# Adjacency layer on one core: contiguous loads, the diagonal found by its column, and three changed orders

## What is computed

```python
x: (8192, 512) float32;  adj: (8192, 8192) float32, symmetric pattern, about 9 entries in a row, diagonal always present
h = relu(layernorm(x))
mask = (adj > 0)
head = mask / max(sqrt(sum(mask * mask, axis=-1)), 1e-12)
inc = adj + head
out = x + (inc @ h) / sum(inc, axis=-1)
```

## Time and profile before

| | before |
|---|---|
| median of 3 runs | 1271.77 us |
| span of the profiled execution (the profile gives no other time of it) | 1276.7 us |
| VectorE busy | 1189.2 us, 93% |
| ScalarE busy | 975.5 us, 76% |
| TensorE busy | 959.0 us, 75% |
| GpSimd busy | 791.1 us, 62% |
| DMA | 471 MB, 369 GB/s over the span |

### The profile page before, as it was taken

The page is one execution under the profiler, slowest core; times in us unless marked ns, Lnnn a source line. Parts: engine busy times, 40 slices in busy tenths (PEclk is TensorE's granted clock), DMA queues, the critical chain, the costliest instruction groups (busy, mean ns, idle before and its releaser), DMA issues.

```text
span 1276.7 us, 14660 instructions
## 1 busy us (share of the span) xinstructions
PE 959.0 (75%) x2680; PEld 478.1 (37%) x2682; DVE 1189.2 (93%) x2868; ACT 975.5 (76%) x1902; POOL 791.1 (62%) x748
## 2 busy tenths in 40 slices
PE   0003878888888878787988887978878888977677
PEld 0001434444444444443434443434444434433343
DVE  6679999998999999998999999999999999999961
ACT  6657787887887988786888877888877888884731
POOL 1003667676666777776766767777776776765562
PEclk9999899898988989899898989999989988987888
DMA  9999999999999999999999999999999999997532
GB/s 356 427 422 406 396 394 388 369 387 369 379 378 382 401 373 401 395 401 394 402 400 401 392 374 384 399 400 395 402 396 402 402 397 373 401 390 275 175 106 74
DMA packets 148207, 471.00 MB, mean 369 GB/s; under 512 B 24826, under 2 KB 24826, under 8 KB 143965
## 3 DMA queue, kind: packets, MB, share of 16 engines
q1 hardware_dynamic: 90368, 331.38, 66.3%
q0 software_dynamic: 57744, 138.64, 29.7%
HBM read 490.47 MB, written 33.82 MB: 411 GB/s over the span
## 4 chain that ended last, share of the span: by engine, by line
DVE 55%; issue 17%; DMA 11%; ACT 6%; PE 6%; another core or an unknown queue 2%; SPq 1%; POOL 0%; DVEq 0%; ACTq 0%; POOLq 0%
DVE cand_word L794 17%; DVE folded L772 16%; DMA adj_tile<-in_adj_dram 8%; DVE cand_index L798 6%; DMA gathered_rows<-in_x_dram 3%; PE acc L1326 3%; DVE cand_index L817 2%; DVE cand_word L812 2%; ACT junk L573 2%; ACT adj_tile L560 2%; ACT diag L636 1%; PE acc L1337 1%; DVE diagonal_alone L779 1%; DVE entry L961 1%
## 5 line engine op out<-in xcount | busy, mean ns | idle before, releaser
L494 POOL DMA_INDIRECT gathered_rows<-h_scratch,slot_column x520 | 559.9, 1077 | 263.1 <-issue 158.0
L573 ACT ACTIVATE junk<-adj_tile,zero_unit 128x2048 bf16<-128x2048 f32 x256 | 510.0, 1998 | 48.3 <-issue 27.5
L1326 PE MATMUL acc<-gathered_rows,diag 128*128 128x512 f32 x1040 | 489.6, 622 | 21.4 <-DMA gathered_rows<-h_scratch,slot_column 18.2
L494 POOL DMA_INDIRECT gathered_rows<-h_scratch,spill_column x198 | 223.1, 1127 | 195.0 <-ACT spill_column L619 135.2
L794 DVE MAX8 cand_word<-folded 128x8 f32<-128x1024 f32 x244 | 298.2, 1222 | 5.9 <-remote 1.3
L772 DVE SCALAR_TENSOR_TENSOR folded<-adj_tile 128x1024 f32<-128x1024 f32 x244 | 296.1, 1214 | 7.7 <-DMA adj_tile<-in_adj_dram 5.6
L1326 PEld LDWEIGHTS acc<-gathered_rows,diag 128*128 128x128 f32 x1040 | 203.8, 204 | 263.4 <-issue 262.6
L798 DVE FIND_INDEX8 cand_index<-cand_word,folded 128x8 uint32<-128x1024 f32 x244 | 297.3, 1219 | 0.0
L1337 PE MATMUL acc<-gathered_rows,spill_matrix 128*128 128x512 f32 x396 | 186.8, 609 | 46.0 <-DMA gathered_rows<-h_scratch,spill_column 42.4
L636 ACT ACTIVATE diag<-ident,weights_and_payload 128x128 f32<-128x128 f32 x581 | 176.2, 388 | 16.0 <-issue 6.5
L1337 PEld LDWEIGHTS acc<-gathered_rows,spill_matrix 128*128 128x128 f32 x396 | 72.8, 192 | 154.8 <-issue 154.6
(11 more groups left out here) (151 smaller groups left out, 880.1 us busy)
## 6 DMA issues: line engine op xcount, KB each, us to landing
adj_tile<-in_adj_dram SPq DMA_DIRECT2D x256, 1024.0 KB
h_scratch<-adj_tile SPq DMA_DIRECT2D x16, 1024.0 KB, 10.6
out_dram<-out_tile SPq DMA_DIRECT2D x64, 256.0 KB
gathered_rows<-in_x_dram SPq DMA_DIRECT2D x12, 1024.0 KB, 12.6
x_residual<-in_x_dram SPq DMA_DIRECT2D x48, 256.0 KB
gathered_rows<-h_scratch,slot_column POOLq DMA_INDIRECT x520
x_held<-in_x_dram SPq DMA_DIRECT2D x4, 1024.0 KB, 7.9
gathered_rows<-h_scratch,spill_column POOLq DMA_INDIRECT x198, 3.5
```

The lines of the kernel that those rows point to most:

```text
L494: nc.gpsimd.indirect_dma_start(out=into, out_offset=None, in_=h[:, :], in_offset=bass.IndirectOffsetOnAxis(ap=column, axis=0), bounds_chec ...
L573: nc.scalar.activation(junk[:, n % 2].rearrange("p (j c) -> p j c", j=2), both[:, :, half], ACT.Relu, bias=zero_unit[:], scale=-UP, accum_ ...
L1326: last = nc.tensor.matmul(acc[t % 3][:], diag[:, t % 2, 1 + s], slot(t % 2, s), start=False, stop=False)
```

## The change

1. A chunk is now 2048 columns that lie together, so each row gives one run of 8 KB. What is folded is the first 1024 of them with the second 1024. SyncE no longer waits for the reading of the diagonal before it reloads a chunk.
2. `read_diagonal`, `cut_diagonal` and `keep_diagonal` are gone. `find_diagonal` compares the columns of the 8 candidates of the diagonal's chunk with the row's own number and sums the value of the one that agrees into the head of `entry_value`; `leave_diagonal` subtracts it from the candidates. `columns_any` runs earlier, `counts`, `ranks` and `columns` later.
3. The extra tile has 4 groups of spilled places, as the wide tiles.
4. TensorE runs `find_owner(t-2)` ahead of `product_spill(t-4)`.
5. `load_x(t)` waits for the residual product and for `row_again` of tile t-2 (the two readers of the buffer) and no longer for `own_done`.
6. The tests of the folded rows lose three small steps, the last marks one.

```diff
-                        if j == diag_chunk(t - 2):
-                            sp.wait_ge(diag_read, t - 1)
-                sp.dma_start(chunk(t % 2, j), adj_h[t // ROWS, t % ROWS, :, :, CW * j:CW * (j + 1)]).then_inc(adj_loaded[t % 2][j], 16)
+                sp.dma_start(A[:, t % 2, 2 * CW * j:2 * CW * (j + 1)],
+                             adj_t[t // ROWS, t % ROWS, :, 2 * CW * j:2 * CW * (j + 1)]).then_inc(adj_loaded[t % 2][j], 16)
...
             def load_x(t):
                 if t >= HELD + 2:
-                    sp.wait_ge(own_done, t - 1)
+                    sp.wait_ge(res_added, t - 1)
+                    if not wide(t - 2):
+                        sp.wait_ge(row_ready, t - 1)
...
-            def read_diagonal(t):
-                nc.vector.scalar_tensor_tensor(out=picked[:], in0=diagonal(chunk(t % 2, diag_chunk(t))[:, diag_half(t)], t),
-                                               scalar=1.0, in1=ident[:], op0=ALU.mult, op1=ALU.mult,
-                                               accum_out=on_diag[:, t:t + 1]).then_inc(diag_read, 1)
-                nc.vector.tensor_tensor(words, words, cap[:], ALU.min).then_inc(diag_cut, 1)
...
+            def find_diagonal(t):
+                dve.wait_ge(cola_ready, t + 1)
+                dve.wait_ge(val_ready, t + 1)
+                nc.vector.scalar_tensor_tensor(out=own_entry[:], in0=in_diag_chunk(cola, t), scalar=diag_column(t),
+                                               in1=in_diag_chunk(val[:, 1:], t), op0=ALU.is_equal, op1=ALU.mult,
+                                               accum_out=val[:, 0:1]).then_inc(diag_found, 1)
+
+            def leave_diagonal(t):
+                dve.wait_ge(diag_found, t + 1)
+                rest = in_diag_chunk(val[:, 1:], t)
+                nc.vector.tensor_tensor(rest, rest, own_entry[:], ALU.subtract).then_inc(diag_left, 1)
...
         def groups(t):
-            return EXTRA if FOLDED <= t < BATCH else FOLDED_EXTRA
+            return EXTRA if wide(t) else FOLDED_EXTRA
...
+                if pay:
+                    find_owner(q)
                 if end:
                     product_spill(f)
-                if pay:
-                    find_owner(q)
```

More of the change, by code:

```diff
@@ L205, in chunk, with diag_column @@
             return A[:, b, 2 * CW * j:2 * CW * (j + 1)].rearrange("p (h c) -> p h c", h=2)
-        def diag_half(t):
-            return t // ROWS * P * ROWS // HALF
         def diag_chunk(t):
-            return t // ROWS * P * ROWS % HALF // CW
-        def diagonal(row, t):
-            first = t // ROWS * P * ROWS % CW
-            return row[:, first:first + P * ROWS].rearrange("p (m j) -> p j m", j=ROWS)[:, t % ROWS]
+            return t // ROWS * P * ROWS // (2 * CW)
+        def diag_column(t):
+            return diag_at[:, t % 16:t % 16 + 1]
         def cands(t):
@@ L247, in searched @@
             return CHUNKS * min(t, FOLDED) + PARTS * max(t - FOLDED, 0)
-        def part(i):
-            return i % 2 * CHUNKS + i // 2
         def paid(t, k):
@@ L801, in part_columns @@
             def part_columns(t, i):
-                if t == BATCH:
-                    return A[:, 0, CW * part(i):CW * (part(i) + 1)]
-                return chunk(t % 2, part(i) % CHUNKS)[:, part(i) // CHUNKS]
+                return A[:, t % 2, CW * i:CW * (i + 1)]
             def part_values(t, i):
@@ L809, in part_values @@
                 else:
-                    dve.wait_ge(adj_loaded[t % 2][part(i) % CHUNKS], 16 * turn(t))
-                e = slice(8 * part(i), 8 * part(i) + 8)
+                    dve.wait_ge(adj_loaded[t % 2][i // 2], 16 * turn(t))
+                e = slice(8 * i, 8 * i + 8)
                 nc.vector.max(out=cv[:, t % 2, e], in_=part_columns(t, i)).then_inc(vals_found, 1)
@@ L976, in period @@
                     values(p)
[L977 removed]
+                    columns_any(p)
                 if pick:
@@ L981, in period @@
                 if small:
-                    counts(p)
+                    find_diagonal(p)
                 if pick:
@@ L986, in period @@
                 if small:
-                    columns_any(p)
-                    ranks(p)
+                    leave_diagonal(p)
                 if pick:
@@ L992, in period @@
                 if small:
+                    counts(p)
+                find_places(t, 1)
+                if small:
+                    ranks(p)
                     columns(p)
-                find_places(t, 1)
                 if small:
@@ L1035, in count_bad @@
                                                     op0=ALU.mult, op1=ALU.add))
-                step(nc.vector.scalar_tensor_tensor(out=z_right[:, on_right], in0=right_diag[:], scalar=ZERO,
-                                                    in1=z_right[:, on_right], op0=ALU.mult, op1=ALU.add))
                 step(nc.vector.tensor_scalar(well[:], z_left[:], ZERO * HALF, None, ALU.is_equal))
@@ L1077, in wide_period @@
                 values(p)
-                keep_diagonal(p)
+                columns_any(p)
                 part_values(t, 1)
                 find_entry(r)
+                if not wide(p):
+                    find_diagonal(p)
                 part_places(t, 1)
+                if not wide(p):
+                    leave_diagonal(p)
+                take_entry(r)
                 counts(p)
-                take_entry(r)
                 if t == FOLDED + 1:
@@ L1315, in residual @@
                     pe.wait_ge(x_loaded[t % 2], 16 * x_turn(t))
-                nc.tensor.matmul(acc[t % 3][:], ident[:], again[:] if t == BATCH else x_of(t), start=True, stop=False)
+                nc.tensor.matmul(acc[t % 3][:], ident[:], again[:] if t == BATCH else x_of(t), start=True,
+                                 stop=False).then_inc(res_added, 1)
                 if not wide(t):
```

54 lines of the change are left out of this document (18 added, 36 removed).

## The result

The changed kernel takes 1284.05 us (median of 4 runs, 1273.14 to 1292.3); the kernel before took 1272.25 us beside it (1271.65 to 1273.69). Some executions of one kernel lie well above its others, and every ratio here leaves those out (the 1292.3 of this result, and one of 1304.1 in c4_early_here), while the medians hold them. The ratio is 1.0058, with a 95% interval from 1.0032 to 1.0085: slower, where 1250 us and faster were forecast. Its profiled execution has a span of 1271.4 us and took 1273.14 us itself, so it is the fastest of the four; that of before (1276.7) lay above its median.

What follows compares the result with a forecast made beforehand. VectorE was taken to bound until tile 50, the DMA engines tiles 51 to 59; -18.7, -4.1 and +1.5 us sum to -21.3, from 1276.7 to 1255.4, or 1250 us for the median; range 1242 to 1269.

Steps and rivals of the forecast that it cites:

- VectorE's edits: On VectorE, diagonal steps and copy removed, two small steps added: 0.39 us a tile saved, bounds 0.10 to 0.45.
- until tile 50 VectorE's own work is the period: In the kernel before, VectorE's 16.94 to 16.95 us a tile sets the time; DMA engines set only tiles 51 to 59.
- the prefetch lasts about as long as it did: In the changed kernel, DMA pace stays 0.57 us a tile above VectorE's, 0.63 before, so loads bind about as late.
- The 8 KB runs: On the matrix loads, 25.7 against 24.6 GB/s an engine: 0.46 us a tile off the DMA pace, bounds nothing to 0.5.
- Rival 2: On the DMA engines, longer runs bring nothing and transfers set tiles 16 to 59: 1268 us, chance 0.20.
- Rival 3: Gathers starve behind 8 KB packets, making TensorE, owners and finally VectorE late: 1277 to 1290 us, chance 0.12.
- The shift costs nothing as long as gathers land: Counts and ranks on VectorE, about 2.4 us later in the period, move other engines' phase without lengthening it.
- The load of x: On SyncE, loads issued earlier by a shorter wait: counted as nothing, worth 3 us if the cover is gone.
- the owners' place: On TensorE, finding owners before the spilled product takes `copy_owner` from behind a gather wait of 42.4 us in all.
- the ends: Tests and wide tiles save 0.5 us, the extra tile's fourth group costs 2 us: +1.5 us.

Runs made afterwards that it cites:

- c4_early_here: Changed kernel with the diagonal's two steps, counts, ranks and columns earlier on VectorE: 1289.4 us, 1.0154 to the kernel before.
- b2_spread: Kernel before with the spilled places of each group dealt over the lanes in another order: 1259.21 us, ratio 0.9923.
- a0_again: The changed kernel itself, unaltered, timed again in another job: 1268.1 us, 0.9990 to the kernel before.
- a1: Changed kernel with the own row waiting only for the product that reads it, not all own products: 1268.5 us, 0.9993 to the kernel before.
- a3: Changed kernel with the diagonal's two steps, counts, ranks and columns earlier on VectorE: 1269.8 us, 1.0006 to the kernel before.
- c1_after_here: The changed kernel itself, unaltered, as yardstick of the last job: 1286.1 us, 1.0109 to the kernel before.
- c2_row_free_here: Changed kernel with the own row waiting only for the product that reads it: 1278.3 us, 1.0039 to the kernel before.
- a4_spread: Changed kernel with the spilled places of each group dealt over the lanes in another order: 1256.3 us, 0.9897 to the kernel before.
- b3_long_spread: Kernel before with 8 KB runs and the spilled places dealt over the lanes: 1259.9 us, ratio 0.9947.
- a8_short_all: Changed kernel with 4 KB runs, spilled places dealt over the lanes, own row's wait narrowed, counts and ranks early: 1250.9 us, 0.9855 to the kernel before.
- c3_short_here: Changed kernel with the old chunks of 4 KB runs: 1274.5 us, 1.0017 to the kernel before.

## Why the prediction was wrong

**VectorE's edits: right in kind, a little large.** The two new steps cost 0.24 us, where 0.16 was taken; the wait of `own_columns` is 0.10 as said. The sum is 0.67 - 0.24 - 0.10 - 0.02 = 0.31 against 0.39. In tiles 3 to 15 VectorE is busy 216.07 us, 220.41 before and 219.71 in b2_spread: 0.28 to 0.33 a tile. Only in those tiles did it reach the time.

**The step that failed: "until tile 50 VectorE's own work is the period", carried over to the changed kernel by "the prefetch lasts about as long as it did".** The two resources lay within 0.3 us a tile of each other, and b2_spread shows that the transfers held tiles 16 to 50 as well, though by only 0.15 us a tile. That left next to nothing for an edit of VectorE, and 0.39 was counted for each tile. The second half hung on the 8 KB runs: without their 0.46 us the prediction's own figures give 17.58 against 16.55, 1.03 us a tile in place of 0.63, and a prefetch that had lasted 35 tiles would be gone after some 21. The changed period of 16.6 us would have wanted 6.78 MB / 16.6 us = 408 GB/s, and 400 is the most that these 44 tiles showed in any run. Tiles 16 to 50 took 603.9 us in place of some 587, VectorE idle for 20.6 us of it. Of the 18.7 us counted for 48 tiles some 4 came, those of tiles 3 to 15.

**The 8 KB runs: wrong, by the whole term.** 25.7 against 24.6 GB/s an engine compared a stretch without gathers with one that has them. The prediction named that as its lower bound ("the difference is the mixing with gathers") and took nearly the upper one. Measured in a stretch with gathers: 24.5 to 25.1 with long runs, 24.2 to 24.7 with short ones, and b1_long_runs, which is this edit alone, no faster than the kernel before (1.0023).

**Rival 2 had the size.** DMA-bound from tile 16, 1268 us, is what a0_again shows (1268.1), and a1 and a3.

**Rival 3 had the sign and the mechanism.** Gathers behind long packets, TensorE late, owners late. It was priced at 1277 to 1290 us with a chance of 0.12; the first runs gave 1284, c1_after_here 1286. The argument against it, that q1 would run out of free buffers and leave the engines to the gathers, did not hold where the transfers set the pace. What the rival didn't count is the slower products after a wait. "The shift costs nothing as long as gathers land" put the weight on the counts; they had no part that a run shows. What closed the circle was an old wait, `row_again` for all own products, which costs 7.8 us in c1_after_here (c2_row_free_here).

**The load of x, the owners' place, the ends: small.** `load_x` and `find_owner` weren't tried apart. From tile 60 to the end it took 161.1 us, 161.9 before, where +1.5 was expected.

**Argued only.** That the diagonal now takes one of the 8 candidate places moves entries from own slots to spilled ones, fills the third group further and could be why the spread gives the changed kernel as much as the kernel before (a0_again to a4_spread 11.8 us, b2_spread 10); it wasn't tried apart. Why the loss is 0.6 to 1.1% in three jobs and none in that of a0_again, when the episodes come in every profile of the changed kernel, is open too.

## What to carry to other kernels

Where two resources are nearly full, neither a small idle time of one nor a full share of the other tells which is the bound: divide the bytes of a step by the best rate that any stretch shows, and compare with the busy time of the engine; the larger is the period, and an edit of the smaller buys nothing beyond the gap. Here that sum says 16.97 us a tile for the transfers before any edit (298.7 MB of tiles 16 to 59 by the rates of the earlier trace rows, over 44, at 400 GB/s), and 16.95 for VectorE.

A lack of bandwidth doesn't stay where it arises. It should fall on a load with prefetch behind it, not on a gather whose consumer is waited for in a circle; so before transfers are made longer, look for such circles and make every wait name its real reader.

## What the hardware showed beyond that

- Which lanes the rows of a partly filled gather fall on matters. Dealing the same rows over all lanes took 10.0 us off the kernel before (0.9923) and raised the rate of 44 tiles from 393 to 400 GB/s, at equal bytes.
- Beside gathers of 2 KB rows, runs of 8 KB move at 24.5 to 25.1 GB/s an engine and runs of 4 KB at 24.2 to 24.7, but TensorE's waits for gathers go from 28.6 to 168.8 us (b2_spread and b3_long_spread).
- One core drew 400 GB/s for 745 us (a8_short_all), above the 358 GB/s that the Trainium skill (DMA: Bandwidth & Descriptors, Where 436 GB/s comes from) names as the limit of a core; the trace disagrees with that for a core that runs alone.
- The issue of a long-run chunk never blocks SyncE for long, that of a short-run chunk does. Issue times of the matrix loads (least, median, longest ns), in the changed kernel and then in c3_short_here, answer to the earlier trace rows:

```profile
L380 SPq DMA_DIRECT2D adj_tile<-in_adj_dram x256: 327/328/1463, 63.1 to 1148.3; - x128
```

```profile
L384 SPq DMA_DIRECT2D adj_tile<-in_adj_dram x256: 367/1255/6695, 62.8 to 1150.0; - x128
```

A chunk of 1 MB is 256 packets of 4 KB or 128 of 8 KB; with the many its issue takes up to 6.7 us, with the few at most 1.5. If it is the room in the queue that holds the short ones back, fewer of their bytes stand ahead of a gather, which would explain the gathers' shorter waits. No run here tests that.
